# The load of x issued by ScalarE's queue instead of SyncE's, in a fused graph-transformer layer

## The reference, cut to what matters

```python
edge_index = jnp.stack([src, dst])
xn = _layernorm(x, axis=-1)
x = x + gnn(xn, edge_index, W1, b1, W2, b2) + mix(xn, w_qkv, mem_kv, w_out, b_out, g_out, g_pre)
x = x + moe(_layernorm(x, axis=-1), router_w, w1, b1, w2, b2)

# gnn: two of these, with a relu between; norm comes from the degrees
def _gcn_conv(x, W, b, src, dst, norm, num_nodes):
    h = x @ W
    msgs = h[src] * norm[:, None]
    return jax.ops.segment_sum(msgs, dst, num_segments=num_nodes) + b
```

## Time and profile before

| | us |
|---|---|
| median of three runs | 755.34 |
| lowest and highest run | 754.62, 762.78 |
| span of the profiled execution | 754.8 |
| TensorE matmul busy | 585.7 (78%) |
| VectorE busy | 509.7 (68%) |
| ScalarE busy | 347.6 (46%) |
| GpSimd busy | 132.2 (18%) |

### The profile page before, as it was taken

The page is one execution under the profiler, slowest core; times in us unless marked ns, Lnnn a source line. Parts: engine busy times, 40 slices in busy tenths (PEclk is TensorE's granted clock), DMA queues, the critical chain, the costliest instruction groups (busy, mean ns, idle before and its releaser), DMA issues.

```text
span 754.8 us, 13942 instructions
## 1 busy us (share of the span) xinstructions
PE 585.7 (78%) x5198; PEld 516.7 (68%) x5198; DVE 509.7 (68%) x1114; ACT 347.6 (46%) x623; POOL 132.2 (18%) x133
## 2 busy tenths in 40 slices
PE   0889791879999999999599999989640499999500
PEld 0245351769999999987499999888530399999500
DVE  6773998459999999818556531299850577887534
ACT  0034773397777777710211111224240388999400
POOL 2000000000000000000000000018886145565600
PEclk9978996799999999999799999999755599999955
DMA  7999999301355531000056867503332245555198
GB/s 186 253 283 284 284 283 313 145 1 54 166 218 219 218 163 58 2 1 1 1 218 271 337 265 297 200 4 84 92 90 76 82 130 138 163 147 151 36 229 280
DMA packets 80158, 121.17 MB, mean 161 GB/s; under 512 B 8573, under 2 KB 68770, under 8 KB 78429
## 3 DMA queue, kind: packets, MB, share of 16 engines
q1 hardware_dynamic: 70621, 107.03, 46.8%
q0 software_dynamic: 9472, 13.27, 5.7%
HBM read 50.00 MB, written 72.21 MB: 162 GB/s over the span
## 4 chain that ended last, share of the span: by engine, by line
PE 48%; DVE 21%; DMA 9%; POOL 8%; issue 6%; ACT 5%; SPq 1%; DVEq 0%; ACTq 0%; POOLq 0%
PE psB L1216 21%; POOL expert_slots L571 8%; DVE hot L683 7%; PE psC L1122 3%; DMA back<-expert_out 3%; PE psC L1216 3%; PE psB L1369 3%; PE psA L1134 3%; DMA xs<-expert_slots 3%; PE psD L1134 2%; DMA acc<-in_x_dram 2%; PE psA L1357 2%; PE psC L1383 1%; ACT counts L1414 1%; PE psD L1383 1%
## 5 line engine op out<-in xcount | busy, mean ns | idle before, releaser
L1216 PE MATMUL psB<-hs,counts 125*128 125x256 f16 x1600 | 210.3, 275 | 3.3 <-DVE hs L790 2.7
L1216 PEld LDWEIGHTS psB<-hs,counts 125*128 125x128 f16 x1600 | 173.0, 140 | 4.9 <-issue 2.8
L683 DVE TENSOR_TENSOR hot<-iota_j,places 128x2048 bf16<-128x2048 bf16 x128 | 154.9, 1223 | 18.0 <-PE psA L1134 12.0
L563 POOL IOTA row_of<- 128x25 f32 x1 | 0.2, 238 | 475.3 <-PE psC L1216 475.3
L578 POOL DMA_INDIRECT expert_out<-y,to_row x64 | 65.8, 1029 | 62.3 <-DVE y L1060 49.4
L1414 ACT CAST counts<-psA 128x1000 f16<-128x1000 f32 x64 | 63.3, 989 | 15.2 <-PE psA L1134 15.2
L571 POOL DMA_INDIRECT expert_slots<-rows,place x50 | 62.1, 1241 | 45.2 <-issue 44.9
L1414 ACT CAST counts<-psD 128x1000 f16<-128x1000 f32 x64 | 63.6, 994 | 12.6 <-PE psD L1134 12.6
L1134 PE MATMUL psA<-hot 128*128 128x125 bf16 x512 | 49.4, 220 | 12.9 <-DVE hot L683 7.1
L1134 PEld LDWEIGHTS psA<-hot 128*128 128x128 bf16 x512 | 38.1, 98 | 22.8 <-DVE hot L683 12.4
L848 DVE TENSOR_TENSOR sum_both<-psB,sum_both 128x256 f32<-128x256 f32 x32 | 13.5, 422 | 57.7 <-ACT sum_both L1474 57.7
(11 more groups left out here) (286 smaller groups left out, 1067.0 us busy)
## 6 DMA issues: line engine op xcount, KB each, us to landing
expert_slots<-zeros SPq DMA_DIRECT2D x8, 3536.0 KB, 29.9
kept_counts<-counts SPq DMA_DIRECT2D x6, 4000.0 KB, 11.4
counts<-kept_counts SPq DMA_DIRECT2D x6, 4000.0 KB, 13.0
xs<-expert_slots SPq DMA_DIRECT2D x32, 272.0 KB, 3.1
back<-expert_out SPq DMA_DIRECT2D x5, 1120.0 KB
w_raw<-in_L_ffn_w_dram SPq DMA_DIRECT2D x2, 2048.0 KB, 11.5
acc<-in_x_dram SPq DMA_DIRECT2D x1, 2800.0 KB
out_dram<-acc SPq DMA_DIRECT2D x5, 560.0 KB
```

Of the source, the lines that this page charges most:

```text
L683: v.tensor_tensor(hot[:, slot].rearrange("p g w n s -> p (g w) n s"), iota_j[:, :, :].unsqueeze(1).to_broadcast([P, 2 * pairs, P, PAIR]), ...
L1216: m = pe.matmul(sum_bank(g, d), counts5[0:PT, buf, a, d, :], hs2[0:PT, a, :, :].rearrange("p q f -> p (q f)"), start=a == 0 and first, sto ...
```

## The change: what it does

The two loads of x leave SyncE's program and become the first two instructions of ScalarE's. They count on the same semaphore. The other loads keep their order on SyncE, and the waits of all engines are as they were. The padding that SyncE waits for ahead of the edges (`pads`) does not concern x, so ScalarE waits for nothing.

```diff
@@ sync
                 sp.dma_start(prev_dst[0:k, c:c + 1], ends[c * P - 1:c * P - 1 + k, :],
                              allow_slow_non_contiguous=True).then_inc(in_edges, 16)
-            for lo, hi in ((0, 112), (112, PT)):
-                sp.dma_start(acc_v[lo:hi], x_v[lo:hi]).then_inc(in_x, 16)
             loads = [
@@ scalar
             sa = Steps(act, scalar_done)
+            for lo, hi in ((0, 112), (112, PT)):
+                act.dma_start(acc_v[lo:hi], x_v[lo:hi]).then_inc(in_x, 16)
             act.wait_ge(var_ok, 1)
```

## The result

The changed kernel is slower; whether by as much as 2% the runs leave open. Its first four runs have a median of 772.26 us (767.80 to 776.11) against 755.78 for the kernel before; the ratio is 1.018, 95% interval 1.011 to 1.025. Six more runs on another occasion gave 768.79 against 757.13: 1.016, 1.012 to 1.021. The forecast, 766.9, had the sign and the wait that decides; its range ended at 769.5, under the median of the first runs. The profiled execution has a span of 768.3 us, 13.5 more than before.

What follows compares the result with a forecast made beforehand. The prediction took an unbroken chain of waits through the engines as the bound, opening with edges and x. It summed 754.8 + (20.2 - 6.65) - 2.0 = 766.35, with 0.5 around it 766.9 us; range 753.5 to 769.5.

Steps and rivals of the forecast that it cites:

- the wait that decides: VectorE's opening wait for the edge loads, 6.65 us before; every microsecond the edges are later was to be lost in full.
- T: Time at which the edges are in, 6.65 us before; forecast at 20.2, with break-even at 8.65.
- the upper side: Case of edges ending behind x on the DMA engines: T = 20.2 taken, up to 22.4; chance 0.57.
- engines divide themselves by packets: DMA engines take the two queues' packets in turn: 1258 of the edges against 625 of x, so x is out first.
- the wait for x goes: VectorE's wait of 4.83 us ahead of the statistics would nearly vanish if the edges were not touched.
- TensorE's tables are late next: On VectorE, the fourth pass would wait for TensorE's last edge table, starting at about 33.3 us instead of 35.23.
- ScalarE's table load costs nothing: At ScalarE's start, two issues delay the table load some 0.87 us, covered by a 36.33 us wait.
- the weights and the zero fill harm nobody: On SyncE, shifted weight loads and zero fill meet no waiting user; nothing was counted for this part.
- With the 0.5 us around it: Time added to the span of 766.35 us to give the measured time, 766.9 us.
- The relief of 2.0 us: On VectorE, the fourth pass gains 35.23 - 33.28, about 2.0 us; 1.0 us if the fourth table takes 3.92.
- Whatever moves the first pass of the statistics' aggregation: A shift of this VectorE pass at 36.37 us moves the end by about the same amount, nothing later being time-fixed.
- the bounds of T: Edges in between 6.65 us, undisturbed, and 22.4 us, ending behind x.

Runs made afterwards that it cites:

- The second trace: The changed kernel profiled again with no edit: edges in at 21.26 us, statistics' aggregation at 49.02 us, fourth edge table 2.85 us.
- the one with the large piece alone: Against the changed kernel, only x's 112-partition piece stays on ScalarE's queue; the 13-partition piece goes on SyncE behind the edges: median 769.60 us, ratio 1.015 to the kernel before.

## Why the prediction was wrong

Right was the mechanism. T, the landing of the edges, decides, and it goes to the upper side. That engines divide themselves by packets, which was only my reading, is borne out by 254 packets against 252, once both queues move; for the first 4 us of x they did not (last section). That the wait for x goes, that TensorE's tables are late next, that ScalarE's table load costs nothing under its long wait, and that the weights and the zero fill harm nobody, stands in the rows above.

That T came out as forecast is partly luck: 20.2 was forecast, 20.34, 21.26 and 20.68 were measured, but two errors in it cancel. The text had x out at 20.2, made late by the edges' bytes, and the edges ending with it. x's last packet starts at 16.92, 16.2 us after its issue, where it was 16.3 us before (5.69 to 22.02): the edges did not delay x. And the edges end some 3 us behind x and not with it: half of their packets were left, as the count of 1258 against 625 had it, first rows of 512 bytes until 18 us and then those of 4 bytes until 20, for which alone the text had allowed up to 2.15 us.

Wrong were the terms around T, each by a little and both one way, and the step by which the range was made.

*"With the 0.5 us around it."* The 0.5 us was the difference between the profiled span and the median of three other runs. A run's own time is 1.75 to 1.87 us above its own span in every run of both kernels for which both are on record. Worth 1.3 us.

*The relief of 2.0 us.* The fourth table took 3.92 us, so the pass waits for it and the relief is 13.69 - 12.81 = 0.9 us. The second trace, with 2.85 us, has 21.26 - 6.65 - (49.02 - 36.37) = 2.0 us. The text had 1.0 us as the other end but summed with the better one.

*"Whatever moves the first pass of the statistics' aggregation (36.37 on VectorE) moves the end by about the same amount."* This is the step that failed, since the range took it as exact. It holds on the average: the three traces of before and of after have their aggregation at 36.52 and 49.24 in the mean, 12.7 us apart, and their spans at 754.1 and 767.9, 13.8 apart. It doesn't hold for one execution, nor for the median of four: what stands behind the aggregation takes 718.4, 719.1 and 715.1 us in the traces of before, 719.1, 720.4 and 716.4 in those of after, and up to 723.4 in the other kernels (the one with the large piece alone). The spans of the changed kernel's runs differ by 11.8 us, those of the kernel before by 8.9 (751.4 to 760.3). Three runs, one at 762.78, had shown such a spread, and the text named it as what a measurement can tell, but the range was made of the bounds of T alone. A forecast of 766.9 with the spread of runs on it would have reached to some 775.

With the first two terms put right (1.3 us, and 1.0 us for the fourth table) the sum is 769.2; the eleven runs of the changed kernel have a median of 769.29. The first four lie 3 us above that, at 772.26, and six more of the same kernel at 768.79, so I put this part down to the spread of the runs. What remains open is why the granted clock is lower in one execution than in another after the opening.

## What to carry to other kernels

Moving a big load to a second queue does not take it out of the way of the small ones: in these traces the queues take turns packet by packet, so many small packets behind or beside few large ones wait until the large ones are out, here 13.7 us for 0.40 MB. If work starts with the small loads, let them land first, and gain time on the big load by waiting for its pieces. Before forecasting within 1%, compare the spread of the runs with the range, not only the bounds of the unknown cost.

## What the runs showed that I had not expected

Packets of the edges did not move at all at first. SyncE issues the edges from 1.15 us, as before, when 828 packets of them went between 2 and 4.5 us. With x issued 0.4 us ahead on the other queue, the traffic of the changed kernel from 1.5 to 5.5 us is x alone:

```profile
DMA packets 199, 1.02 MB, mean 255 GB/s; under 512 B 0, under 2 KB 0, under 8 KB 199
...
q10 hardware_dynamic: 199, 1.02, 93.4%
```

So a load issued 0.4 us sooner has some 4 us of the engines to itself before the turns begin. Where the edge loads wait in that time no view shows. And the time by which a queue's issue is held can be long: the three last loads of prev_dst held SyncE for 15.10 us in the changed kernel, against 1.77 before, though they carry a kilobyte.
